# Attention pass of a four-layer graph network: sixteen batches of gathered rows instead of eight

## The reference

```
q, k, v = (x @ W + b).reshape(n, 4, 32)           # for Wq, Wk, Wv
score   = einsum('ehc,ehc->eh', q[dst], k[src]) / sqrt(32)
m       = segment_max(score, dst)
p       = exp(score - m[dst])
denom   = segment_sum(p, dst)
out     = segment_sum(v[src] * (p / denom[dst]), dst)
x_r     = x @ Wskip + bskip
beta    = sigmoid(concat([out, x_r, out - x_r]) @ Wbeta)
x       = layernorm(x + beta * x_r + (1 - beta) * out)
```

## Time and profile before

| | |
|---|---|
| median of 3 runs | 6286.65 us |
| the profiled execution, its own time | 6292.27 us |
| its span, first to last instruction | 6290.4 us |
| attention pass, from POOL's first gather to DVE's last `weigh` | 4765.6 to 6147 us of the span |
| PE, DVE, ACT, POOL busy over the span | 58%, 55%, 24%, 62% |
| granted TensorE clock, mean | 0.64 of full speed |

### The profile page before, as it was taken

How to read it: one execution, slowest core, us unless ns; L and a number is a source line. 1 busy time by engine, 2 the same in 40 slices (tenths; PEclk the granted TensorE clock), 3 DMA queues, 4 the chain that set the end, 5 groups by cost and what they waited for, 6 DMA issues and landing times. The chain is left out here.

```text
span 6290.4 us, 85261 instructions
## 1 busy us (share of the span) xinstructions
PE 3618.6 (58%) x19084; PEld 2770.9 (44%) x19084; DVE 3432.9 (55%) x6723; ACT 1540.3 (24%) x3649; POOL 3883.9 (62%) x4265
## 2 busy tenths in 40 slices
PE   3444333344555555544777777767744677676763
PEld 2333222232333333333555555556633555555551
DVE  4544222224766666643666666678954455555554
ACT  1110010131222222222222222248841122222224
POOL 6666566656566666656566666668965555555552
PEclk7555555566777777765555555569966666666666
DMA  5555444424555556524555555569954555555551
GB/s 175 167 160 155 140 156 156 156 64 132 170 177 177 175 179 178 178 76 124 144 150 149 150 150 153 150 183 302 313 160 144 158 166 166 163 170 166 165 159 56
DMA packets 810665, 1008.50 MB, mean 160 GB/s; under 512 B 230951, under 2 KB 516017, under 8 KB 810548
## 3 DMA queue, kind: packets, MB, share of 16 engines
q1 hardware_dynamic: 460628, 459.45, 24.8%
q0 software_dynamic: 144320, 323.10, 18.8%
q10 hardware_dynamic: 205600, 224.71, 10.2%
HBM read 645.12 MB, written 361.71 MB: 160 GB/s over the span
## 5 line engine op out<-in xcount | busy, mean ns | idle before, releaser
L518 POOL DMA_INDIRECT L_gath<-tab_kv,src x832 | 789.4, 949 | 572.0 <-issue 243.9
L518 POOL DMA_INDIRECT L_gath<-tab,src x832 | 793.8, 954 | 475.2 <-issue 236.7
L518 POOL DMA_INDIRECT L2a_gath<-tab_h,src x832 | 790.1, 950 | 478.0 <-issue 249.2
L518 POOL DMA_INDIRECT L_gath<-in_x,src x832 | 789.4, 949 | 463.9 <-issue 233.9
L653 ACT ACTIVATE L_back<-L_pB 128x512 f32<-128x512 f32 x624 | 367.8, 590 | 1284.5 <-remote 744.7
L636 DVE TENSOR_TENSOR_SCAN L_acc<-L_mask,L_acc,L_pT 128x512 f32<-128x512 bf16 x207 | 264.4, 1278 | 725.5 <-remote 498.1
L624 PE MATMUL L_pB<-ident,L_acc 128*128 128x128 f32 x2496 | 519.1, 347 | 104.8 <-ACT L_back L653 85.4
L624 PEld LDWEIGHTS L_pB<-ident,L_acc 128*128 128x128 f32 x2496 | 406.2, 184 | 291.1 <-issue 279.9
L1249 PE MATMUL L_pR<-L_pv,L_same 128*128 128x132 f32 x1664 | 378.1, 396 | 267.2 <-DVE L_pv L1327 147.2
L582 PE MATMUL L_pT<-ident,L_gath 128*128 128x128 f32 x832 | 219.5, 417 | 516.1 <-DMA L_gath<-in_x,src 369.3
L853 PE MATMUL L_pM<-L_hid,w_W 128*128 128x512 f32 x416 | 326.3, 878 | 310.9 <-DVE L_acc L890 178.2
(11 more groups left out here) (292 smaller groups left out, 7619.2 us busy)
## 6 DMA issues: line engine op xcount, KB each, us to landing
run<-L_back ACTq DMA_DIRECT2D x416, 256.0 KB
L_seed<-seed SPq DMA_DIRECT2D x416, 256.0 KB
run<-L_back ACTq DMA_DIRECT2D x208, 264.0 KB
seed<-L_zeros SPq DMA_DIRECT2D x208, 256.0 KB
sent<-L2a_gath ACTq DMA_DIRECT2D x208, 256.0 KB
L_sent<-sent SPq DMA_DIRECT2D x208, 256.0 KB
run<-L_back SPq DMA_DIRECT2D x208, 256.0 KB
L_mask<-same SPq DMA_DIRECT2D x208, 128.0 KB
```

Of the source, the lines that this page charges most:

```text
L518: gp.indirect_dma_start(out=gath[k][:, t, :], out_offset=None, in_=table, in_offset=bass.IndirectOffsetOnAxis(ap=g["src"][:, tile:tile + 1 ...
```

## The change

The ring `gath` gets 16 batches (`LONG = 2 * DEEP`), so 64 KB of each SBUF partition instead of 32 KB. POOL's room wait now looks 16 batches back. DVE's loop is written out 16 batches long; those of its steps that keep buffers in 8, 4 or 2 slots get their slot and round numbers through `on_deep`, and their waits are the same as before. The loops of PE, ACT and SP stay. The buffer `heads` (3.5 KB of each partition) goes; the tiles' first queries are fetched into the buffers `back`, four columns each, and written to `seed` by seven DMAs of one column instead of two. The pace wait, its `behind` of 5 and the 32 unpaced batches stay.

```diff
-    rings = DEEP // SLOTS
+    rings, LONG = DEEP // SLOTS, 2 * DEEP
+    on_deep = lambda f: lambda n, k, r: f(n, k % DEEP, r * (LONG // DEEP) + k // DEEP)
     with Phase(nc, "L3") as ph:
-        gath, s_gath, s_go = edge_buffers(ph, 2 * D)
+        gath, s_gath, s_go = edge_buffers(ph, 2 * D, LONG)
...
-        heads = ph.sb("heads", [P, -(-TILES // P), D])
+        head_at = lambda c: back[c // BT][:, c % BT, 0:D]
...
-            sp.dma_start(g["seed"][0:whole * P, :].rearrange("(c p) f -> p c f", p=P), heads[:, 0:whole, :]).then_inc(s_headw, 16)
-            sp.dma_start(g["seed"][whole * P:TILES, :], heads[0:odd, whole, :]).then_inc(s_headw, 16)
-            sp.wait_ge(s_headw, 32)
+            for c in range(whole + 1):
+                count = P if c < whole else odd
+                sp.dma_start(g["seed"][c * P:c * P + count, :], head_at(c)[0:count, :]).then_inc(s_headw, 16)
+            sp.wait_ge(s_headw, 16 * (whole + 1))
...
-                gp.indirect_dma_start(out=heads[0:count, c, :], out_offset=None, in_=g["tab_q"],
+                gp.indirect_dma_start(out=head_at(c)[0:count, :], out_offset=None, in_=g["tab_q"],
...
-                need(v, s_probe, r * rings + k // SLOTS)
+                need(v, s_probe, r * (LONG // SLOTS) + k // SLOTS)
...
-            pipeline(v, BATCHES, DEEP, [(0, pairs), (1, times_key), (1, dot), (2, on_groups(softmax)), (6, weigh), (11, on_groups(gaps)), (12, on_groups(joined))])
+            pipeline(v, BATCHES, LONG, [(0, on_deep(pairs)), (1, times_key), (1, on_deep(dot)), (2, on_deep(on_groups(softmax))), (6, weigh),
+                                        (11, on_deep(on_groups(gaps))), (12, on_deep(on_groups(joined)))])
```

## The result

The changed kernel takes 6332.07 us (median of 4 runs, 6329.96 to 6343.1) where the kernel before takes 6287.45 on the same chip: ratio 1.0077, 95% interval 1.0059 to 1.0094. It is 45 us slower; 6240 and faster was forecast. The profiled execution took 6343.1 us, its span is 6341.2.

What follows compares the result with a forecast made beforehand. Taken as bound by a ring of waits, PE's results coming out when POOL pauses (245 us of pauses). Paced pauses -47, other terms 0: profiled 6292.3 to 6245, less 5.6 for the median: 6240 us, range 6180 to 6335.

Steps and rivals of the forecast that it cites:

- Room wait, removed: POOL's paced gathers: looking 16 batches back, all 55 waits for `weigh` go, removing 168 us before new pauses are counted.
- Three pauses for five batches at 1.8 us: POOL's paced stretch: taken as 1.6 batches to a pause, 110 pauses x 1.8 = 198 us against 245: -47 us.
- the case that the prediction named as wrong as a whole: POOL's gather line: waits for `weigh` remain, or the number of pauses falls and each grows longer.
- My walk: One round followed through POOL's pauses with PE's and DVE's durations: two batches, one, two, so 1.67 to a pause.
- The start: Batches 8 to 31: POOL's early lead is given back at batch 32; taken as 0, bounds +20 and -20 us.
- Rival A: Paced stretch: one batch to a pause, 176 pauses, +72 us, 6359; chance 0.30.
- Rival B: Paced stretch: two batches to every pause, 88 pauses x 1.67, -98 us, 6189; chance 0.15.
- DVE's loop: DVE, 11 turns of 16 batches instead of 22 of 8: 0, at most -3 us.
- first queries: SP's seven writes instead of two: first seed load 2.8 us later, hidden by DVE's preparation, so 0.
- Rival C: POOL's wait only changes its name, as many stops, just as long: within 12 us of 6287; chance 0.12.
- Its near relation: DMA queues: more queued gathers delay SP's seed loads by taking queue share; at most turns the gain into Rival C.
- The rule on SBUF's ports: By it running ahead with gathers would be free; the prediction went by the profile's rows, which disagreed in time.

Runs made afterwards that it cites:

- e11: Changed kernel with SP's rim loads one batch step earlier (lag 11 instead of 12), computation complete: 6226.71 us, ratio 0.9917 to the kernel before.
- e14: Changed kernel with SP's rim loads two batch steps earlier (lag 10): 6170.99 us, ratio 0.9943 to the kernel before.
- e15: Kernel of e11 with the pace wait one batch looser (`behind` 9): ratio 0.9953 to the kernel before.
- e17: Kernel of e11 with the pace wait one gather earlier (`behind` 4): ratio 0.9957 to the kernel before.
- e8: Changed kernel, SP loading the rim rows of the group before, without waiting for the group's own stores; late results: ratio 1.0072 to the kernel before.
- e7: Changed kernel with the room wait 8 back to batch 31, 16 back from batch 32; late results: ratio 1.0075 to the kernel before.
- e6: Changed kernel with the room wait 8 back again, ring of 16 kept; late results: ratio 1.0001 to the kernel before.
- e10: Changed kernel with SP's rim-load step thinned to one wait with one increment, first group's rims loaded each time: 6258.48 us, ratio 0.9962 to the kernel before.
- e1: Changed kernel with the room wait 8 back again, ring of 16 kept, without late results: 5215.99 us, ratio 1.0001 to the kernel before.
- e4: Changed kernel, SP loading the rim rows of the group before, without late results: 5211.56 us, ratio 0.9994 to the kernel before.
- e18: Kernel of e11 once more, without late results: 5214.28 us, ratio 1.0002 to the kernel before.
- e12: Kernel before with SP's rim loads one batch step earlier (lag 11): 6274.63 us, ratio 0.9994 to the unedited kernel before.
- e2: Changed kernel with the room wait 8 back to batch 31, 16 back from batch 32, without late results: 5215.15 us, ratio 0.9996 to the kernel before.

## Why the prediction was wrong

- *Room wait, removed.* Right as a mechanism: no room wait is left in the paced stretch, and the pause at 4m+1 shrank from 4.40 to 1.90 in the round shown, 71 us in all.
- *Three pauses for five batches at 1.8 us.* This step failed, and with it the sum. It came out as 94 pauses of 3.10, 291 us, where I had 110 of 1.8, 198 us; from 101 pauses of 2.42 that is fewer and longer ones, the case that the prediction named as wrong as a whole. My walk followed PE and DVE from row to row and gave SP's group step no time. But in the rows of before that step is done right at POOL's restart; the room wait's 2.8 us from the release to the restart are the time in which SP gets its loads out. Restarting at the release puts the step among the gathers, where it takes 5.1 us instead of 2.3, and PE meets the rims in order ahead of the L1208 that POOL waits for. Without that, e11 has 102 pace waits with 211.6 us behind the one of batch 32, 1.77 us of excess each and 1.72 batches to a pause, where I had 110, 1.8 and 1.6. Its ratio times 6287 is 6235; with those of e14, e15 and e17 it would be 6251 to 6260. The forecast was that of a kernel in which SP's step does not bind.
- *The start.* Forecast 0 within 20 us, as POOL would give back its lead at batch 32; it does, in the wait of 28.81 us. The trace gives +7 (230.4 against 223.2), and e8 with the burst +12 on e7 without it (234.8 against 222.3; e8 has the edit of the rim loads as well). Yet e8 with 6349.94 us is not slower than e7 with 6353.66: as time it can't be told from 0. That DVE's first `pairs` wouldn't move was wrong: it came 7 us later.
- *DVE's loop, first queries.* The five writes more put SP's first load back by 2.8 us, as worked out. Both are hidden: e6 at 1.0001 holds them and the longer ring.
- *Rival A* (one batch to a pause) did not happen: 1.86. (Its upper end is worked out wrong: 72 and the start's 20 are +92, not +97.) *Rival B* had the number of pauses nearly right (88 against 94) and their length at 1.67 where 3.10 was measured. *Rival C* fell: fewer stops, and not within 12 us. Its near relation, SP's loads held up by the gathers, was the right place on the wrong grounds: I wrote that no row shows PE waiting for a load, while PE's waits of before had 13.8 us in 6 for `L_rim`, a view that I hadn't read by line. It is not a matter of the DMA queues' shares: the time is lost ahead of the loads' issue, and e10 and e11, which win it back, move as many bytes.
- *The rule on SBUF's ports* ("SBUF — State Buffer" of the Trainium skill, section "SBUF: two separate sides"), that transfers can't slow the engines, agrees with e1 to e4 and e18, where the pass's gathers take 1040 us whichever batch the room wait looks at. Where results are late, as in the earlier trace rows, running ahead was not free: it cost 45 us. Whether a port has any part in that no run shows, so there the rule is neither borne out nor refuted.

## What to carry to other kernels

A wait that looks like pure loss may be the window in which some third engine gets its work done. Before taking it out, list what every engine does between the release and the restart, SP's and ACT's queues among them, and put each item after the restart in the walk. Then move the item that gets late (here one lag in SP's pipeline) together with the wait: the lag alone gave 0.9994 (e12), the longer ring alone 1.0077 (the first comparison), both together 0.9917 (e11, in e12's group).

## What the runs showed of the hardware

- The same kernel took 5214 us or 6209 to 6305 us, each steady within a group of runs, and on one chip both were met. In the slower condition the gather passes are long (the first one's last gather at 1257.4 us against 1059.9 in e1) and results of PE come out microseconds late (L1214 of the earlier trace rows ends at 5403.29 and is used at 5406.92). A ratio from one condition doesn't carry to the other.
- In the slower condition SP is slow too once POOL has streamed gathers for some us. In the kernel before, the step of five waits with increments ahead of the rim loads takes 0.7 us in 5 of the 7 groups where POOL stands, and 1.9 to 2.2 in the 29 groups where SP comes to it 0.6 to 1.0 us behind POOL's restart. In e8, all five waits long fulfilled, it takes 2.7 to 8.3 us in the 30 groups where SP comes to it 3.0 to 3.3 us behind the restart, 5.4 or more in 25 of them. It is neither the waits nor the increments as such: SP's plain register moves too go from 0.07 to 0.72 us (medians up to 2 us, and 4 to 8 us, behind the restart). In e2 and e18 they take 0.07 throughout.
- What makes SP slow and PE's results late, and what sets the condition, no run here tells.
